# A four-layer graph network on one core: the edge attributes are transposed in the first layer and stored turned, instead of being transposed in the message layer

## The chip, the cores and the metric

One core of one Trainium2 chip. The metric is the device time of one execution of the whole kernel, in microseconds (us); it was taken in several runs, of which the median is given. Lower is better.

## What is computed

A graph of N = 3125 nodes and 50,000 edges, sorted by destination, goes through four layers with a layer norm ahead of each and a residual behind it:

```
x: (3125, 64)   src, dst: (50000,)   edge_attr: (50000, 32)
layer 0  typed:     agg[n] = sum over edges into n of  h[src] @ W[type],  16 types
layer 1  mean:      h[n] @ W_r + mean over edges into n of h[src] @ W_l
layer 2  message:   m = silu([h[src], h[dst], edge_attr] @ w1 + b1) @ w2 + b2
                    agg[n] = sum of m;  h[n] = LN(h[n] + mlp([h[n], agg[n]]))
layer 3  attention: 8 edge types, keys from h[src], h[dst] and active rules,
                    softmax over the edges into n, weighted sum of values
```

The part of `w1` that multiplies the edge attributes has 32 rows, so each edge needs one product of 32 numbers with a 32 x 64 matrix.

## The kernel before

**Tiles.** The sorted edges are cut into tiles of 128. A pair of an edge tile and a node tile (128 nodes) that it has edges into is a slot: 416 slots in G = 52 groups of SG = 8. The groups are also cut in four chunks, `PIECES` = (16, 16, 12, 8) groups. Every layer that sums over edges runs over the 52 groups. All five engines run their own program over them, in an order that is written out by hand, and meet in semaphores with a number per group.

**One group.** POOL gathers eight tiles of 128 rows (L583, one indirect DMA each) from a table in memory: row i of a tile is the table's row for edge i's source. They lie in a ring of eight groups; before it fills a place again it waits, in the first two layers, for PE's sum of an earlier group (`used`), in the message layer for DVE's adds (`edge_sum`). DVE makes the one-hots of a group (`oh`, L785: 128 edges by 128 nodes for each slot) in one of two buffers, for which it waits for the sum two groups back. PE multiplies the one-hots with the gathered rows and adds into the sums of the nodes in its own memory (eight matmuls by slot, recorded as sixteen; L1388 in the first two layers, L1353 in the message layer), and then signals `used`.

**The message layer** adds for each group: SP loads the slots' node numbers once for all partitions (`drow`, L518) and the edge attributes (`ea`, L514); DVE makes transposed one-hots from the former (`ohT`, L791); PE transposes the attributes (`ea_T`, two transposes, L1502, signal `eaT_ps`), ACT copies them to SBUF (`take_ea`, L1203, signal `eaT_sb`), and PE multiplies them with `w1c` (two matmuls, L1509) and adds the destination's part by the one-hots (L1511), signal `eb_ps`; DVE adds the gathered source part (L960, signal `edge_sum`), ACT applies Silu (L1209, signal `silu`), and PE sums (L1353). The programs run ahead of each other: at group g PE transposes for g + 2, makes the edge products of g + 1 and sums g. The program's names for both the gathered tiles and the attributes are parts of one buffer, `flat`, in the records.

**The attributes' way to memory.** The message layer needs the attributes of whole edge tiles by slot. In the first layer, behind the gathers of groups 12, 22, 32 and 42 (`TAKE_EA`), POOL gathers one chunk's attributes (L594): each of up to 128 partitions gets one slot's 128 x 32 numbers, 16 KB. SP stores them as they are in `edge_attr_by_slot` (L497, four stores). The message layer loads them from there with the edges over the partitions: 1024 pieces of 128 B for a group.

**The first layer** gathers typed rows from a table of nodes by types, except in the first twelve groups (`WHOLE`), for which plain rows have been gathered ahead, and PE does transposes and typed products (`turned0`, `typed0`) while the table isn't there yet.

## Time and profile before

| | |
|---|---|
| median of 3 runs | 2665.6 us |
| lowest and highest | 2657.2, 2675.9 us |
| span of the profiled execution | 2690.8 us |
| busy: PE, DVE, ACT, POOL | 1523.2, 1051.5, 487.3, 1543.2 us |
| DMA packets, data moved | 159861, 159.26 MB |

The profiled execution is one more execution than the three of the median; nothing but its span is recorded of it, so that the rows of the trace are to be held against 2690.8 us. An engine's busy time is that of its instructions; a DMA that POOL or SP issues is not in their busy time except for POOL's building of an indirect DMA, which the rows show as an instruction of POOL.

The page of the profile cuts the span in slices; two of its rows, for orientation, are PE's and POOL's, where each digit is one fortieth of the span in tenths of busy time:

```
PE   5545332424478888765376667659553536445564
POOL 5447766764667777735566666662344556665620
```

The first layer's gathers lie in slices 3 to 10, the message layer's in 19 to 27, the last layer's from 33 on.

### The profile page before, as it was taken

To read this page: it belongs to the slowest core of one execution; us is meant where nothing else is said; L and a number is where in the kernel's file an instruction comes from. 1 tells how busy PE (TensorE), PEld (TensorE's weight loads), DVE (VectorE), ACT (ScalarE), POOL (GpSimd) and SP (SyncE) were. 2 spreads that over 40 slices of the span, in tenths; PEclk is the share of its full clock that TensorE was granted. 3 is DMA by queue.
4 is the path that set the end of the run, shared out by engine and by line. 5 is a ranking of instruction groups with operands and counts; after the bars stand their busy time and mean duration, and the time that the engine had idled before them with its cause. 6 is when DMAs were issued, how large, how long until landed. Compare 5 with 4: busy or idle time off the path is not lost.

```text
span 2690.8 us, 27765 instructions
## 1 busy us (share of the span) xinstructions
PE 1523.2 (57%) x8443; PEld 1343.0 (50%) x8443; DVE 1051.5 (39%) x2213; ACT 487.3 (18%) x1153; POOL 1543.2 (57%) x1509
## 2 busy tenths in 40 slices
PE   5545332424478888765376667659553536445564
PEld 2224332424367777765376666658332325435554
DVE  4446110111556565633122222223524634334467
ACT  2100000000356666501000000001211111001020
POOL 5447766764667777735566666662344556665620
PEclk8656555555677777766555655657656766666677
DMA  6432122120111111103122222222341212222210
GB/s 199 130 110 86 24 84 58 36 61 16 30 31 36 34 37 34 33 12 65 37 52 50 57 51 51 58 51 44 110 162 52 65 54 66 61 55 68 58 39 13
DMA packets 159861, 159.26 MB, mean 59 GB/s; under 512 B 108361, under 2 KB 111993, under 8 KB 158748
## 3 DMA queue, kind: packets, MB, share of 16 engines
q1 hardware_dynamic: 111372, 89.07, 11.7%
q0 software_dynamic: 48352, 68.42, 11.5%
q8 instruction: 79, 1.29, 0.2%
q14 instruction: 58, 0.48, 0.1%
HBM read 118.71 MB, written 46.06 MB: 61 GB/s over the span
## 4 chain that ended last, share of the span: by engine, by line
another core or an unknown queue 30%; DVE 21%; PE 17%; issue 16%; POOL 10%; DVEq 2%; ACT 1%; DMA 1%; SPq 1%; ACTq 0%; POOLq 0%
POOL flat L583 10%; DVE flat L824 7%; PE ps L1353 4%; DVE oh L785 2%; DVE oh L1043 2%; PE ps L1388 2%; PE ps L1511 2%; DVE msg L1034 2%; DVEq L333 1%; PE ps L1341 1%; DVE msg L960 1%; DVE ohT L791 1%; PE ps L1325 1%; PE ps L1509 1%
## 5 line engine op out<-in xcount | busy, mean ns | idle before, releaser
L583 POOL DMA_INDIRECT flat<-table,flat x1061 | 1122.8, 1058 | 639.7 <-issue 314.7
L1388 PE MATMUL ps<-flat,oh 128*128 x1664 | 328.9, 380 | 368.1 <-DVE oh L785 255.3
L785 DVE TENSOR_TENSOR oh<-iota_n,drel 128x1024 f32<-128x1024 f32 x156 | 190.1, 1223 | 867.8 <-remote 605.0
L1388 PEld LDWEIGHTS ps<-flat,oh 128*128 128x128 f32 x1664 | 314.3, 291 | 394.7 <-issue 392.7
L583 POOL DMA_INDIRECT flat<-table,tile_idx x359 | 346.7, 966 | 267.9 <-DVE base L1037 140.2
L1353 PE MATMUL ps<-msg,oh 128*128 128x64 f32 x832 | 173.3, 393 | 156.5 <-ACT msg L1209 135.4
L1353 PEld LDWEIGHTS ps<-msg,oh 128*128 128x128 f32 x832 | 166.6, 304 | 160.4 <-issue 160.4
L1366 PE MATMUL ps<-uvT,flat 128*128 128x192 bf16 x2200 | 229.3, 275 | 25.7 <-ACT flat L1191 17.2
L1366 PEld LDWEIGHTS ps<-uvT,flat 128*128 128x128 bf16 x2200 | 219.8, 112 | 34.6 <-issue 29.3
L1576 PE MATMUL ps<-qn,ohT 128*128 x832 | 159.0, 349 | 124.9 <-issue 104.0
L1511 PEld LDWEIGHTS ps<-uvT,ohT 128*128 128x128 f32 x832 | 178.3, 291 | 64.3 <-issue 48.9
L1576 PEld LDWEIGHTS ps<-qn,ohT 128*128 128x128 f32 x832 | 143.4, 258 | 132.7 <-issue 132.1
L824 DVE TENSOR_TENSOR flat<-flat,iota_node 128x1536 bf16<-128x1536 f32 x110 | 193.2, 1757 | 3.0
L1511 PE MATMUL ps<-uvT,ohT 128*128 x832 | 166.1, 361 | 48.2 <-issue 48.2
L1187 ACT ACTIVATE flat<-flat,iota_node 128x512 bf16<-128x512 f32 x220 | 146.8, 714 | 170.8 <-DMA flat<-tile_source 105.5
L1585 PE MATMUL ps<-flat,oh 128*128 128x65 f32 x704 | 115.0, 329 | 70.7 <-DVE oh L1043 45.5
L1585 PEld LDWEIGHTS ps<-flat,oh 128*128 128x128 f32 x704 | 112.6, 248 | 76.2 <-issue 76.2
L1191 ACT ACTIVATE flat<-flat 128x512 bf16<-128x512 bf16 x220 | 126.4, 621 | 3.5
L1260 ACT COPY flat<-flat 128x64 f32 x416 | 65.8, 241 | 271.7 <-DMA flat<-table,tile_idx 209.3
L1032 DVE COPY rule_e<-ps 128x32 f32<-128x32 f32 x52 | 9.8, 188 | 269.2 <-remote 225.1
L1203 ACT COPY flat<-ps 128x256 f32<-128x256 f32 x52 | 19.3, 373 | 528.4 <-remote 360.4
L1509 PE MATMUL ps<-flat 128*128 128x256 f32 x208 | 105.0, 602 | 9.7 <-issue 9.4
(320 smaller groups left out, 1481.9 us busy)
## 6 DMA issues: line engine op xcount, KB each, us to landing
table<-flat SPq DMA_DIRECT2D x52, 512.0 KB
drow<-slot_node SPq DMA_DIRECT2D x104, 256.0 KB
flat<-table,flat POOLq DMA_INDIRECT x1061
flat<-edge_attr_by_slot SPq DMA_DIRECT2D x52, 128.0 KB
edge_attr_padded<-edge_attr SPq DMA_DIRECT2D x1, 6250.0 KB
flat<-table,tile_idx POOLq DMA_INDIRECT x359
flat<-tile_source SPq DMA_DIRECT2D x22, 256.0 KB
edge_attr_by_slot<-flat SPq DMA_DIRECT2D x2, 2048.0 KB
```

What stands on the lines that cost most here:

```text
L583: nc.gpsimd.indirect_dma_start(dest(t % PLACES), None, table, at_).then_inc(tile_gat[k % TRING], 16)
L785: V.tensor_tensor(oh[:, b], iota_n[:].unsqueeze(1).broadcast_to([P, SG, P]), drel[:, g * SG:(g + 1) * SG].unsqueeze(2).broadcast_to([P, SG ...
L824: V.tensor_tensor(src_oh[:, m % BINS, 0:ON_DVE, :], src_row[:, b].unsqueeze(1).broadcast_to([P, ON_DVE, PICK * P]), iota_node[:, CH * c:CH ...
L1187: last = A.activation(src_far[:, k - ON_DVE], src_row[:, q % 2], ACT.Square, bias=iota_node[:, t:t + 1], scale=-1.0)
L1191: last = A.activation(src_oh[:, m % BINS, k, :], src_far[:, k - ON_DVE], ACT.Relu, bias=1.0, scale=-1.0)
L1353: last = T.matmul(acc[:, bass.ds(n[j] * D, D)], oh[:, b, j, :], rows_[:, j, :], start=False, stop=True, skip_group_check=True)
L1366: last = T.matmul(picked_ps[b][:, j], src_oh[:, m % BINS, k, j * P:(j + 1) * P], h_parts[:, :, t, :], start=(t == 0 and j % 2 == 0), stop= ...
L1388: last = T.matmul(acc[:, bass.ds(n[j] * pitch + shift, width)], oh[:, b % 2, j, :], got[:, bass.ds(place[j], width)], start=False, stop=Tr ...
L1509: T.matmul(eb[b % 2][:, 256 * q:256 * q + 256], eaT[:, b % 2, q, :], w1c.rearrange("p s d -> p (s d)"), start=True, stop=False, skip_group ...
L1511: last = T.matmul(eb[b % 2][:, j * D:(j + 1) * D], ohT[:, b % 2, j, :], v[:, bass.ds(n[j], 1), :].rearrange("p t d -> p (t d)"), start=Fal ...
L1576: last = T.matmul(qr_ps[g % 2][:, j // 4, j % 4], ohT[:, b % 2, j, :], qn_room[:, bass.ds(n[j] * QR, P)], start=True, stop=True)
L1585: last = T.matmul(acc[:, bass.ds(n[j] * PITCH + SHIFT, W)], oh[:, b % 2, j, :], values[:, bass.ds(lw * SG + j, 1), :].rearrange("p s d -> ...
```

## The change

It has three parts.

- The message layer loses `ea_T` on PE, `take_ea` on ACT and their two semaphores. SP's load `ea_in` fills `eaT` itself, with 1 KB for each partition, from a new array `edge_attr_turned` that has one block of 128 x 256 for each group. It waits for `eb_ps`, the edge products two groups back, where it had waited for the transposes two groups back (`eaT_ps`).
- The first layer gets `turn_ea` on PE: 58 steps of four transposes, by way of four rooms in PSUM, and 58 copies on ACT. A chunk has eight steps (`TURNS`) that read the gathered rows with a stride of 32 numbers and turn them from "slot by edge" to "edge by slot" for one attribute each, and then one step for two groups that turns blocks of 4 slots by 32 attributes to the form that the product wants. Two steps stand behind the sum of a group, for the groups from TAKE_EA + 2 on: 14 to 21, 24 to 31, 34 to 40 and 44 to 49. The steps of a group wait for the copy of four steps back.
- SP's four stores become 26 of 256 KB, each behind its step's copy; POOL's gather of the next chunk's attributes waits for the chunk's eighth step (`ea_turned`) instead of for the store; PE waits for the last copy before it goes on to the nodes.

```diff
@@ SP
             for c in range(SC):
-                sp.wait_ge(s("ea_taken"), 16 * (c + 1))
-                sp.dma_start(ea_slot_d[START[c]:START[c] + ROWS_OF[c], :], ea_rows[0:ROWS_OF[c], :]).then_inc(s("ea_slot_out"), 16)
+                for k in range(PIECES[c] // 2):
+                    pair_ = FIRST[c] // 2 + k
+                    sp.wait_ge(s("ea_moved"), ea_steps_before(c) + TURNS + k + 1)
+                    sp.dma_start(eaT_d[2 * pair_:2 * pair_ + 2].rearrange("g p k -> p g k"), turned_ea[:, pair_ % 2, :].rearrange("p (g k) -> p g k", g=2)).then_inc(ea_out[pair_ % 2], 16)
...
             def ea_in(g, b):
-                sp.wait_ge(s("eaT_ps"), g + 1)
-                sp.dma_start(ea[:, b, :].rearrange("e (s d) -> e s d", s=SG), ea_slot_d[g * SG:(g + 1) * SG, :].rearrange("s (e d) -> e s d", d=ED)).then_inc(eas[b], 16)
+                sp.wait_ge(s("eb_ps"), g + 1)
+                sp.dma_start(eaT[:, b].rearrange("p q k -> p (q k)"), eaT_d[g]).then_inc(eas[b], 16)
@@ POOL, in the first layer, at the groups of TAKE_EA
                     if c:
-                        pool.wait_ge(s("ea_slot_out"), 16 * c)
+                        pool.wait_ge(s("ea_turned"), ea_steps_before(c - 1) + TURNS)
@@ ACT, first layer
+            for i, (c, k) in enumerate(EA_STEPS):
+                act.wait_ge(s("ea_turned"), i + 1)
+                if k < TURNS:
+                    A.copy(by_edge[:, 0:ROWS_OF[c], 4 * k:4 * k + 4], room[i % 4].rearrange("p (d s) -> p s d", d=4)[:, 0:ROWS_OF[c], :]).then_inc(s("ea_moved"), 1)
+                else:
+                    pair_ = FIRST[c] // 2 + k - TURNS
+                    if pair_ >= 2:
+                        act.wait_ge(ea_out[pair_ % 2], 16 * (pair_ // 2))
+                    A.copy(turned_ea[:, pair_ % 2, :], room[i % 4]).then_inc(s("ea_moved"), 1)
@@ ACT, message layer
-            def take_ea(g, b):
-                act.wait_ge(s("eaT_ps"), g + 3)
-                act.wait_ge(s("eb_ps"), g + 1)
-                A.copy(eaT[:, b % 2], tp[b % 2][:, 0:2 * P].rearrange("p (q k) -> p q k", q=2)).then_inc(s("eaT_sb"), 1)
-
             def step2(g, b, left):
-                if left > 2:
-                    take_ea(g + 2, b)
@@ PE, first layer
+            def turn_ea(i, c, k):
+                if i == 0:
+                    pe.wait_ge(s("ahead_read"), 4 * WHOLE[0] + 1)
+                if i >= 4:
+                    pe.wait_ge(s("ea_moved"), i - 3)
+                if k == 0:
+                    pe.wait_ge(s("ea_taken"), 16 * (c + 1))
+                if k == TURNS:
+                    pe.wait_ge(s("ea_moved"), i)
+                n = ROWS_OF[c]
+                for j in range(4):
+                    if k < TURNS:
+                        last = T.transpose(room[i % 4][:, j * P:j * P + n], ea_rows[0:n, :].rearrange("s (e d) -> s d e", d=ED)[:, 4 * k + j, :], ident[0:n, 0:n])
+                    else:
+                        at_ = 4 * (4 * (k - TURNS) + j)
+                        last = T.transpose(room[i % 4][:, j * P:(j + 1) * P], by_edge[:, at_:at_ + 4, :].rearrange("p s d -> p (s d)"), ident[:])
+                last.then_inc(s("ea_turned"), 1)
...
                     if l == 0 and g + 2 < WHOLE[0]:
                         turned0(g + 2)
+                    if l == 0:
+                        for i in ea_steps_at(g):
+                            turn_ea(i, *EA_STEPS[i])
@@ PE, message layer
-            def ea_T(g, b):
-                pe.wait_ge(eas[b % 2], 16 + (g - b % 2) * 8)
-                for q in range(2):
-                    last = T.transpose(tp[b % 2][:, q * P:(q + 1) * P], ea[:, b % 2, q * P:(q + 1) * P], ident[:])
-                last.then_inc(s("eaT_ps"), 1)
-
             def edges2(g, b, n):
                 pe.wait_ge(s("ohT"), g + 3)
-                pe.wait_ge(s("eaT_sb"), g + 1)
+                pe.wait_ge(eas[b % 2], 16 + (g - b % 2) * 8)
...
-                if left > 2:
-                    pe.wait_ge(s("eaT_sb"), g + 1)
-                    ea_T(g + 2, b + 2)
```

The order of instructions shows it at three places. First, PE in the first layer, between the sum of group 18 and that of group 19, before the change. The names: `flat` is here the buffer of the gathered rows, `ps` PE's sums, TENSOR_LOAD a read of the slots' numbers, ISA the setting of an address.

```order
L1388 MATMUL ps<-flat,oh 128x65
L333 TENSOR_LOAD flat x2
L1388 ISA [waits tiles_gathered3,ahead_done,oh]
L1388 MATMUL ps<-flat,oh 128x65
L1388 ISA
L1388 MATMUL ps<-flat,oh 128x65
```

The same place with the change:

```order
L1422 MATMUL ps<-flat,oh 128x65
L1401 MATMUL ps<-ident,flat 128x128 [waits ea_moved]
L1401 MATMUL ps<-ident,flat 128x128 x3
L1401 MATMUL ps<-ident,flat 128x128 [waits ea_moved]
L1401 MATMUL ps<-ident,flat 128x128 x3
L334 TENSOR_LOAD flat x2
L1422 ISA [waits tiles_gathered3,ahead_done,oh]
L1422 MATMUL ps<-flat,oh 128x65
```

Eight transposes and two waits for ACT's copies have come between the two sums. The second place is PE in the message layer, from the end of one group's sum to the edge products of a later one, before the change:

```order
L1353 MATMUL ps<-msg,oh 128x64
L333 TENSOR_LOAD flat
L1502 MATMUL ps<-ident,flat 128x128 [waits ea_in0,eaT_sb]
L1502 MATMUL ps<-ident,flat 128x128
L1509 MATMUL ps<-flat 128x256 [waits eaT_sb,ohT,edge_sum]
L1511 ISA
```

And with it:

```order
L1368 MATMUL ps<-msg,oh 128x64
L334 TENSOR_LOAD flat
L1541 MATMUL ps<-flat 128x256 [waits ea_in1,ohT,edge_sum]
L1543 ISA
L1543 MATMUL ps<-uvT,ohT 128x64
```

The two transposes are gone, and the products wait for the load itself where they waited for ACT's copy. The third place is SP at the beginning of the message layer, before the change:

```order
L518 DMA drow<-slot_node 128x1024 [waits ohT,ea_slot_out]
L514 DMA flat<-edge_attr_by_slot 128x8x32 [waits eaT_ps]
L518 DMA drow<-slot_node 128x1024 [waits ohT]
L514 DMA flat<-edge_attr_by_slot 128x8x32 [waits eaT_ps]
```

And with it:

```order
L532 DMA drow<-slot_node 128x1024 [waits ohT,turned_ea_out1,turned_ea_out0]
L528 DMA flat<-edge_attr_turned 128x256 [waits eb_ps]
L532 DMA drow<-slot_node 128x1024 [waits ohT]
L528 DMA flat<-edge_attr_turned 128x256 [waits eb_ps]
```

The loads keep their places; what the attributes' load waits for is the edge products in place of the transposes, and it stands ahead of the next group's `drow` on the same queue.

## Rows read from the trace of the kernel before

**Rows 1.** The page, its top and part 1: busy us (share of the span) x instructions

```profile
span 2690.8 us, 27765 instructions
...
PE 1523.2 (57%) x8443; PEld 1343.0 (50%) x8443; DVE 1051.5 (39%) x2213; ACT 487.3 (18%) x1153; POOL 1543.2 (57%) x1509
```

**Rows 2.** Windows by stage: stretch, length, busy PE PEld DVE ACT POOL, PEclk, DMA share, GB/s

```profile
186.00:652.00 466.00, 173.14 (x751) 151.03 (x750) 98.28 (x80) 1.87 (x7) 328.63 (x324) 0.52 0.22 53
1237.00:1816.00 579.00, 360.44 (x1624) 340.37 (x1624) 126.69 (x427) 43.66 (x88) 374.11 (x372) 0.55 0.26 52
1816.00:1880.00 64.00, 58.61 (x336) 55.99 (x335) 25.32 (x94) 8.92 (x17) 16.85 (x15) 0.70 0.24 46
```

**Rows 3.** Timeline of 1464 to 1482: start, duration, engine, operation, count [idle before <-releaser]

```profile
1464.93 3.62 PE L1353 MATMUL ps<-msg,oh 128*128 128x64 f32 x16
...
1468.34 0.63 PE L1502 MATMUL ps<-ident,flat 128*128 128x128 f32 x2
...
1475.04 0.94 POOL L583 DMA_INDIRECT flat<-table,flat  x1 [0.30 <-issue]
...
1478.40 1.22 DVE L785 TENSOR_TENSOR oh<-iota_n,drel 128x1024 f32<-128x1024 f32 x1 [15.73 <-remote]
1478.44 0.37 ACT L1203 COPY flat<-ps 128x256 f32<-128x256 f32 x1 [15.77 <-remote]
...
1480.95 1.21 POOL L583 DMA_INDIRECT flat<-table,flat  x1 [4.97 <-DVE msg L960]
```

**Rows 4.** Waits of POOL; windows 1230:1845, 186:282 (two rows), 282:652, 2147:2581

```profile
POOL flat L583 <- DVE msg L960: 95.7, 18, 18.1
...
POOL flat L583 <- issue: 22.9, 62, 4.3
POOL flat L583 <- remote: 4.4, 1, 4.4
...
POOL flat L583 <- remote: 25.1, 5, 7.6
...
POOL flat L583 <- DVE base L1037: 103.7, 16, 19.7
```

**Rows 5.** Timeline of the first layer, around 464 and behind its last gather

```profile
464.19 1.23 DVE L785 TENSOR_TENSOR oh<-iota_n,drel 128x1024 f32<-128x1024 f32 x1 [38.68 <-remote]
464.43 1.82 POOL L583 DMA_INDIRECT flat<-table,flat  x1 [5.59 <-remote]
...
652.54 17.32 PE L1388 MATMUL ps<-flat,oh 128*128 x80 [21.61 <-DVE oh L785]
```

**Rows 6.** Timeline at the start of the message layer

```profile
1273.37 0.37 PE L1502 MATMUL ps<-ident,flat 128*128 128x128 f32 x1 [2.42 <-issue]
...
1331.90 1.21 POOL L583 DMA_INDIRECT flat<-table,flat  x1 [18.06 <-DVE msg L960]
```

**Rows 7.** Timeline behind POOL's last gather of the message layer

```profile
1848.54 0.63 PE L1502 MATMUL ps<-ident,flat 128*128 128x128 f32 x2
1848.97 1.06 PE L1509 MATMUL ps<-flat 128*128 128x256 f32 x2
```

**Rows 8.** Waits of PE in 1237:1880, and the timeline of one attributes' load

```profile
PE ps L1353 <- ACT msg L1209: 135.4, 25, 10.0
...
1236.99 0.43 SPq L514 DMA_DIRECT2D flat<-edge_attr_by_slot  x1
...
1240.72 0.41 PE L1502 MATMUL ps<-ident,flat 128*128 128x128 f32 x2 [0.74 <-DMA flat<-edge_attr_by_slot]
```

**Rows 9.** Timeline of a shorter pause of the message layer

```profile
1677.79 1.23 DVE L785 TENSOR_TENSOR oh<-iota_n,drel 128x1024 f32<-128x1024 f32 x1 [14.31 <-remote]
...
1680.35 1.21 POOL L583 DMA_INDIRECT flat<-table,flat  x1 [3.55 <-DVE msg L960]
```

**Rows 10.** SP's queue in 1430:1780 and 2222:2550: packets, MB, share of 16 engines

```profile
q1 hardware_dynamic: 33152, 11.01, 15.9%
...
q1 hardware_dynamic: 3744, 6.82, 7.6%
```

More of the change, by code:

```diff
@@ L66, in network @@
         drel_d = dram("slot_node", (SLOTS, P), bf16)
-        ea_slot_d = dram("edge_attr_by_slot", (SLOTS, P * ED))
+        eaT_d = dram("edge_attr_turned", (G, P, SG * ED))
         src_d = dram("tile_source", (SC * P, P))
@@ L190, in network @@
         ohT = sb("ohT", [P, 2, SG, P])
-        ea_room = early(P, [2 * SG * ED])
-        ea = ea_room.rearrange("p (b k) -> p b k", b=2)
+        eaT = early(P, [2, 2, P])
         src_oh_at = taken[0]
-        eaT = early(P, [2, 2, P])
         msg = sb("msg", [P, 2, SG, D])
@@ L208, in network @@
         assert 2 * R0 * D == 2 * SG * P
+        by_edge = flat[:, taken[0]:taken[0] + P * ED].rearrange("p (s d) -> p s d", d=ED)
         pack = early(P, [SC, 4, P], i32)
@@ L276, in network @@
         pre2 = early(P, [NT, D])
+        turned_ea = pre.rearrange("p t d -> p (t d)")[:, 0:4 * SG * ED].rearrange("p (b k) -> p b k", b=2)
         src_rows = early(P, [SC, P])
@@ L325, in network @@
         eas = [s("ea_in0"), s("ea_in1")]
+        ea_out = [s("turned_ea_out0"), s("turned_ea_out1")]
         tab = [s(f"table_out{b}") for b in range(4)]
@@ L376, in network, with ea_steps_before, ea_steps_at @@
         TAKE_EA = (12, 22, 32, 42)
+        TURNS = ED // 4
+        def ea_steps_before(c):
+            return sum(TURNS + n // 2 for n in PIECES[0:c])
+        EA_STEPS = [(c, k) for c in range(SC) for k in range(TURNS + PIECES[c] // 2)]
+        def ea_steps_at(g):
+            return [i for i, (c, k) in enumerate(EA_STEPS) if g == TAKE_EA[c] + 2 + k // 2]
         def groups(eng, step):
@@ L519, in drow_in @@
                              .rearrange("p (s k) -> p s k", s=SG)).then_inc(drows[b], 16)
-            sp.wait_ge(s("ea_slot_out"), 16 * SC)
+            for b in range(2):
+                sp.wait_ge(ea_out[b], 16 * G // 4)
             for g in range(G):
@@ L901, in _ @@
             link(V.tensor_tensor(pre2, pre2, row("L2_gnn_b3"), ALU.add))
+            for b in range(2):
+                dve.wait_ge(ea_out[b], 16 * G // 4)
             for k, (t0, t1) in enumerate(HALVES):
@@ L912, in _ @@
             dve.wait_ge(s("drel_out"), 16 * SC)
-            dve.wait_ge(s("ea_slot_out"), 16 * SC)
             dve.sem_inc(s("stage_over"), 1)
@@ L1198, in _ @@
             take_transposed(hT)
-            def take_ea(g, b):
-                act.wait_ge(s("eaT_ps"), g + 3)
-                act.wait_ge(s("eb_ps"), g + 1)
-                A.copy(eaT[:, b % 2], tp[b % 2][:, 0:2 * P].rearrange("p (q k) -> p q k", q=2)).then_inc(s("eaT_sb"), 1)
             def step2(g, b, left):
-                if left > 2:
-                    take_ea(g + 2, b)
                 act.wait_ge(s("edge_sum"), g + 2)
                 A.activation(msg[:, b % 2], msg[:, b % 2], ACT.Silu).then_inc(s("silu"), 1)
-            take_ea(0, 0)
-            take_ea(1, 1)
             groups(act, step2)
@@ L1295, in _ @@
             pe.sem_inc(s("used"), 2)
-            pe.sem_inc(s("eaT_ps"), 2)
             pe.sem_inc(s("eb_ps"), 2)
@@ L1458, in _ @@
             gathered_sums(0)
+            pe.wait_ge(s("ea_moved"), len(EA_STEPS))
             node_transposes(h[:], *both("h", 3))
@@ L1528, in step2 @@
                 sum_into_nodes(b % 2, n, msg[:, b % 2])
-            ea_T(0, 0)
-            ea_T(1, 1)
             edges2(0, 0, tiles_of[0])
```

## The prediction

> **What bounds the kernel now.** I read four views in this order: the page's busy times, the windows by stage, the waits of POOL, and the timeline of one pair of groups. POOL and PE are each busy for 57% of the span, so neither explains it alone [rows 1]. By stage [rows 2] the two parts that the change touches are the gathers of the first layer (186 to 652) with the sums behind them, and the message layer: 579 us until POOL's last gather, then 64 us in which PE finishes. One gather takes 0.94 us and the next starts 0.30 us later, so a group of eight costs POOL 10 us, and with a pause of 4.97 us a pair of groups takes some 25 [rows 3]. POOL is the pacemaker there, and what it loses are its pauses: 18 of them, 95.7 us, between one run of gathers and the next [rows 4].
>
> What ends a pause is seen in the timeline [rows 3]. PE's sum of a group runs from 1464.93 for 3.62 us, so it ends at 1468.6, and PE goes on at once with transposes and edge products. But DVE, which waits for the semaphore of that sum (`used`) and for nothing else, starts its one-hots only at 1478.40, 9.8 us later, and ACT, which waits for the transposes of 1468.34, starts its copy at 1478.44. Both start 2.4 us after POOL's sixteenth gather has ended (1475.04 plus 0.94). Only DVE's adds, behind them, let POOL go on, at 1480.95: a pause of 4.97 us. So while POOL gathers without a break, PE's finished work becomes known late. The first layer has the same: one-hots that wait for a sum start at 464.19, 38.68 us after DVE's last work, and POOL resumes at 464.43 after 5.59 us [rows 5]. At the start of the message layer it is visible in PE itself: a transpose of 0.37 us (1273.37) stands 2.42 us behind the record before it, 2.8 us from start to start, where two of them take 0.63 us elsewhere [rows 3], and that stretch ends in the longest pause, 18.06 us [rows 6]. I can't name the mechanism from this trace. What I can count is how often it bites: 18 pauses in 52 groups with 38 PE matmuls each by the code (1976; the two windows have 1624 and 336 records [rows 2], a few are missing), 5 pauses in the 41 groups or so of the first layer after its twelfth (282 to 652), with 16 each, and 1 pause named so in the 96 us before, where the typed products of the first twelve groups come on top [rows 4].
>
> **Message layer: what goes.** Per group two transposes of PE, one copy of ACT (0.37 us [rows 3]), and two handovers (PE to ACT, ACT to PE). PE's two transposes cost little of its time: the product behind them starts 0.43 us later (1848.54 to 1848.97), with the clock at 0.70 in that window [rows 2, 7].
> (a) While POOL gathers, this time is off the path: PE waits for ACT's Silu 135.4 us in the layer, and what the transposes themselves wait for, the attributes' load, ends 0.74 us of waiting once [rows 8]. Worth 0.
> (b) After POOL's last gather PE is the bound (busy 58.61 of 64 us [rows 2]), for some six groups of which four or five still have transposes: 4.5 times 0.43. **Minus 2.**
> (c) In the slow stretch at the start two transposes stand between the sum of one group and the edges that the next adds need. At 2.8 us each they cost 5.6 us. **Minus 3**, bounds 0 and 5.6.
> (d) The pauses. They have two usual lengths: 4.97 us [rows 3] and 3.55 us [rows 9], 1.4 us apart. In the short one DVE was released 1.0 us after POOL's last gather (1676.80 to 1677.79), in the long one 2.4. Between the first release of a pair and its second PE has 54 matmul records (sum, transposes, edges, sum: 16, 2, 20, 16); after the change 52. If the late release is a queue of finished work, two records fewer bring it forward by something between nothing and the 1.4 us of the two lengths, for the 17 pauses behind the first. The third of the bounds is that all pauses go: 95.7 us. Against a large gain speaks the last layer: it has no attributes and no transposes at all and still 16 pauses with 103.7 us [rows 4]. I take 0.8 us for each of 17, the middle of 0 and 1.4 rounded up: **minus 14**, bounds 0 and 95.7.
>
> **Message layer: what moves.** The attributes' load now waits for `eb_ps`, the edge products two groups back, where it waited for transposes two groups back; and the one-hot load of the next group is queued behind it on SP. By the pair of [rows 3] the edges of a pair end at about 1473 and are known at 1478.4; the load that this frees lands some 4 us later (the load issued with the group at 1236.99 was what PE waited for until 1240.72 [rows 8]), and the products that read it start a sum, an edge block and a sum later, two sums of 3.62 us alone [rows 3]. So over 7 us stand against some 4. The one-hot load behind it has the same slack. Cost 0; if the cover failed in each group it would be some 2 us a group, 100 us, which I take up in the rivals' tail, not in the sum.
> The load itself shrinks from 1024 pieces of 128 B to 128 of 1 KB. In 350 us of the layer SP's queue moved 33152 packets and held 15.9% of the DMA engines; in 328 us of the last layer, without attributes, 3744 packets and 7.6% [rows 10]. That work goes from engines that are busy for a quarter of the time and are waited for by nobody: 0. The Trainium skill, page "DMA: Bandwidth & Descriptors", section Specifications, says that a transfer needs pieces of at least 512 B for line rate. By that rule the load gets cheaper, and if the layer followed its DMA time the saving would be the 8.3 points between the two shares, some 50 us of 643. The trace gives the rule no place to act, because only 0.7 us of waiting ends on that load; I keep it as a reason for the fast rival, no more.
>
> **First layer: what is added.** 58 steps of four transposes, 232 in all, in groups 14 to 49, two steps behind the sum of a group; 58 copies of 128x512 on ACT, which is idle there (1.87 us busy of 466 [rows 2]), at twice the 0.37 us of one half as wide [rows 3], 43 us in all beside the gathers; 26 stores of 256 KB in place of 4 of up to 2 MB; and waits: PE for ACT's copies, POOL for the eighth step of a chunk before it gathers the next chunk's attributes.
> (e) Where PE is not the bound, 8 transposes a group at 0.21 us (half of the 0.43) are 1.7 us in a group of 10 to 11, with PE 37% busy (173 of 466) [rows 2]: 0. Half of them read their rows with a stride of 32 elements, which no row of this trace does. Bounds: 0.21 us, as contiguous ones, and three times that, 5.1 us a group; even so PE fits beside 10 us.
> (f) At the end PE is the bound: five sums stand back to back behind the last release (652.54, 17.32 us) [rows 5]. The steps of groups 47 to 49, and perhaps of 46, now stand between them: 24 to 32 transposes at 0.21 us. **Plus 6.** PE's new wait for the last copy costs nothing, since two sums follow the last step. SP's loads of the next layer are queued behind the last store; it comes two sums ahead of this layer's end, and the first of them is wanted only behind the normalisation of the nodes: 0.
> (g) Release of finished work. 24 records a group in place of 16. After the twelfth group 5 pauses with 25.1 us stand in 370 us; in the 96 us before, with about 25 records a group, 1 with 4.4 and one more that the view puts under issue, of 4.3 [rows 4]. The denser part thus has two pauses in 11 groups, 0.18 a group, the thin part 5 to 7 in 40, some 0.13 to 0.17. The difference, up to 0.06 for 29 groups, is 1.7 pauses of 4.4 us: **plus 8**. Bounds: 0, and the message layer's rate of 18 in 52, 0.35 a group, which makes 6 more pauses of 5 us, 30.
> (h) POOL's wait for the eighth step: its tile gathers of that group had waited for the sum just ahead of the step, 10 us earlier. Between 0 and 5 us at each of three places; I take 0, since the gatherer would have paused a group later anyway.
>
> **The sum.** Minus 2, minus 3, minus 14, plus 6, plus 8: minus 5 on a profiled span of 2690.8 us. That execution is 0.9% above the median of the runs, 2665.6, and there is nothing else to take its surroundings from; I scale the difference with it and predict 2661 us. A measurement of this kernel, with runs from 2657.2 to 2675.9, tells about 1% from no change.
>
> **The rivals.**
> A, clearly faster: the pauses of the message layer go for the most part, because PE no longer stands between its sums with a handover to ACT, and because 46,600 small packets leave the queues. For it: in the pauses ACT's copy and DVE's one-hots are released within 0.04 us of each other [rows 3], so the copy is part of what is late. Against: the last layer's 16 pauses. Half of 95.7 us, with (b) and (f) to (g): minus 5 more than minus 35 and down to minus 85: 2575 to 2630, say 2615.
> B, slower: the added steps bring the first layer into the state of [rows 6]. It is one mechanism: PE issues one record in 2.8 us while POOL gathers, the eighth step waits for a copy that waits for a release, the sums behind it stand, and POOL pauses for 18 us in place of 5. It happens if the steps are dense enough to fill whatever fills at the start of the message layer; four chunks at 13 us more give plus 52, together with the rest 2705 to 2720. From two such places on it outweighs the message layer's gain. Against: the first twelve groups of this layer have as many records and show no such stretch.
> C, the message layer gains nothing but (b), since its rhythm is POOL's and the last layer's equals it, and the first layer pays (f) and (g): plus 12, 2677. That is within 1%, as is my forecast.
> D, that the change doesn't do what it says: the transposes are gone from the message layer, as the order of instructions shows, so this is only the case of DMA time that nobody waited for; it gives C's time.
>
> **How the numbers follow.** Forecast and C together 0.60, A 0.25, B 0.15. Faster by over 1% 0.25, within 1% 0.60, slower 0.15. The range goes from 2612, which leaves out the lower part of A, to 2702, which leaves out most of B.
>
> **What the changed profile would show.** The windows of the message layer 15 to 20 us shorter, its pauses fewer than 18 or shorter than 95.7 us in sum; no wait for the attributes' load in PE's list; the same pace of about 25 us a pair. In the first layer 232 more transposes, POOL's pauses at 35 to 40 us in sum in place of 29.5, and 23 us in place of 17.3 behind the last release. Wrong would be the forecast if the first layer's pauses grow by more than 30 us, if transposes with the long stride take over 1 us each, or if the message layer's pauses vanish.

## The result, and the profile after

The changed kernel takes 2683.45 us in the median of 20 runs, the kernel before, timed with it, 2667.46 us in the median of 20. The ratio is 1.0073, with a 95% interval of 1.0042 to 1.0103: slower by 0.7%. That is inside what I had called no change and inside the range, but I had forecast the other sign (minus 5 us), and the interval excludes it. One of the two profiled executions is unusual and the other isn't: the kernel before was profiled at a span of 2690.8 us, far above its median, the changed one at 2681.3, near its own. So the two spans say nothing of the change, and what follows compares stretches. The experiments further down ran on two chips, the first and the third series on one and the second on another, and the kernel before has another median on each; every run is compared with the kernel before on its own chip. Some executions fell in a slower state of the chip: the ratios leave them out, the medians don't.

The top of the page and its part 1, changed kernel:

```profile
span 2681.3 us, 27979 instructions
...
PE 1565.1 (58%) x8571; PEld 1381.6 (52%) x8571; DVE 1051.3 (39%) x2213; ACT 500.8 (19%) x1159; POOL 1538.0 (57%) x1509
```

PE has 128 matmuls more (8571 against 8443 in [rows 1]; 232 were added and 104 taken away), and is busy 42 us longer. At 0.24 us a transpose (1.94 us for eight, L1401 at 324.96) 128 of them are worth 31 us, so some of the 42 us are something else. The windows by stage, the same three as [rows 2] (stretch, length, busy time of PE, PEld, DVE, ACT, POOL, then PE's granted clock, DMA share, GB/s):

```profile
186.00:652.00 466.00, 208.22 (x993) 182.88 (x992) 101.94 (x84) 30.54 (x61) 326.63 (x324) 0.56 0.21 50
1237.00:1816.00 579.00, 379.20 (x1579) 354.85 (x1580) 128.54 (x433) 27.16 (x43) 380.86 (x377) 0.51 0.23 52
1816.00:1880.00 64.00, 54.20 (x227) 51.19 (x225) 20.58 (x70) 4.44 (x7) 10.79 (x11) 0.50 0.15 40
```

The second row is the one to read. PE executed 1579 matmuls where it had executed 1624, and was busy longer for them, 379 us in place of 360. The granted clock had been 0.55 there and is 0.51; in the third window it had been 0.70 and is 0.50, the lower level, all the time. POOL's waits, in the order of [rows 4], for windows 1225:1845, 282:655 (three rows) and 2147:2581 (two rows):

```profile
POOL flat L598 <- DVE msg L976: 88.5, 18, 16.9
...
POOL flat L598 <- remote: 29.7, 7, 5.8
POOL flat L598 <- PE ps L1422: 6.0, 1, 6.0
POOL flat L609 <- remote: 4.0, 1, 4.0
...
POOL flat L598 <- DVE base L1053: 78.3, 15, 9.2
...
POOL flat L598 <- ACT flat L1276: 5.2, 1, 5.2
```

The message layer's pauses have hardly changed (88.5 us against 95.7). Those of the first layer after its twelfth group are 39.7 us in sum against 25.1. The last layer, in which no instruction differs, has 83.5 us in its two rows against 103.7 before, 20 us less: so much do pauses differ from one execution to another.

Then what had no row ahead of the prediction: the time from POOL's last gather of the message layer to its first of the next layer. It stands in brackets behind POOL's next gather, as the idle time before it. Timeline, first of the kernel before, then of the changed one; the rows of PE are the sums of groups behind POOL's last gather:

```profile
1845.13 3.62 PE L1353 MATMUL ps<-msg,oh 128*128 128x64 f32 x16
1853.98 3.62 PE L1353 MATMUL ps<-msg,oh 128*128 128x64 f32 x16
1861.95 1.95 PE L1353 MATMUL ps<-msg,oh 128*128 128x64 f32 x16
1867.13 1.99 PE L1353 MATMUL ps<-msg,oh 128*128 128x64 f32 x16 [0.40 <-ACT msg L1209]
1872.34 1.99 PE L1353 MATMUL ps<-msg,oh 128*128 128x64 f32 x16 [0.40 <-ACT msg L1209]
...
1920.29 0.95 POOL L571 DMA_INDIRECT uvT<-table,flat  x1 [82.23 <-DMA table<-h]
```

```profile
1862.85 3.62 PE L1368 MATMUL ps<-msg,oh 128*128 128x64 f32 x16
1871.38 3.62 PE L1368 MATMUL ps<-msg,oh 128*128 128x64 f32 x16
1879.91 3.62 PE L1368 MATMUL ps<-msg,oh 128*128 128x64 f32 x16
...
1934.59 0.94 POOL L586 DMA_INDIRECT uvT<-table,flat  x1 [104.36 <-DMA table<-h]
```

From one sum to the next is one group. Before, the first group took 8.85 us and the later ones 5.2, since the granted clock rose in the middle: it is 0.50 from 1840 to 1860 and 1.00 from 1865 to 1880. In the changed kernel each takes 8.53 us to the end. The 0.32 us that the removed transposes saved per group at the half clock is there; the 3.3 us per group that the full clock had given is gone. The stretch is 22 us longer: 104.36 in place of 82.23. Two things are in these 22 us. PE had seven sums left behind POOL's last gather before and eight in the changed kernel, which is one group or 8.5 us; the other 13 or so are four groups at 3.3 us, the clock.

### The profile page after: what moved, and what is told of

Its sections match the earlier page's. It is cut to its first block, busy times and chain, and to the rows that moved or that the text cites. A ratio compares the mean times of both kernels' runs of the same rounds, so it can differ in the third digit from the quotient of the medians.

```text
span 2681.3 us, 27979 instructions
## 1 busy us (share of the span) xinstructions
PE 1565.1 (58%) x8571; PEld 1381.6 (52%) x8571; DVE 1051.3 (39%) x2213; ACT 500.8 (19%) x1159; POOL 1538.0 (57%) x1509
## 4 chain that ended last, share of the span: by engine, by line
another core or an unknown queue 33%; DVE 22%; PE 19%; issue 17%; POOL 5%; DVEq 2%; ACT 1%; DMA 1%; SPq 1%; ACTq 0%; POOLq 0%
DVE flat L839 6%; POOL flat L598 5%; PE ps L1368 4%; PE ps L1422 3%; DVE oh L800 3%; PE ps L1543 2%; DVE oh L1059 2%; DVE msg L1050 1%; DVEq L334 1%; PE ps L1541 1%; PE ps L1603 1%; DVE ohT L806 1%; PE ps L1340 1%; PE ps L1356 1%
## 5 line engine op out<-in xcount | busy, mean ns | idle before, releaser
L1422 PE MATMUL ps<-flat,oh 128*128 x1664 | 316.9, 362 | 279.2 <-DVE oh L800 146.9
L1422 PEld LDWEIGHTS ps<-flat,oh 128*128 128x128 f32 x1664 | 303.8, 277 | 303.4 <-issue 300.3
L1368 PE MATMUL ps<-msg,oh 128*128 128x64 f32 x832 | 187.6, 419 | 119.8 <-ACT msg L1227 117.0
L1543 PEld LDWEIGHTS ps<-uvT,ohT 128*128 128x128 f32 x832 | 198.9, 321 | 91.9 <-issue 75.8
L1368 PEld LDWEIGHTS ps<-msg,oh 128*128 128x128 f32 x832 | 180.8, 329 | 124.7 <-issue 124.7
L1543 PE MATMUL ps<-uvT,ohT 128*128 x832 | 186.6, 391 | 66.5 <-issue 66.4
L1227 ACT ACTIVATE msg<-msg 128x512 f32<-128x512 f32 x52 | 32.9, 632 | 636.1 <-DVE msg L976 514.8
L1612 PEld LDWEIGHTS ps<-flat,oh 128*128 128x128 f32 x704 | 108.7, 240 | 80.1 <-issue 80.0
L1541 PE MATMUL ps<-flat 128*128 128x256 f32 x208 | 119.3, 666 | 23.5 <-issue 22.9
```

The lines of the kernel that those rows point to most:

```text
L1368: last = T.matmul(acc[:, bass.ds(n[j] * D, D)], oh[:, b, j, :], rows_[:, j, :], start=False, stop=True, skip_group_check=True)
L1422: last = T.matmul(acc[:, bass.ds(n[j] * pitch + shift, width)], oh[:, b % 2, j, :], got[:, bass.ds(place[j], width)], start=False, stop=Tr ...
L1541: T.matmul(eb[b % 2][:, 256 * q:256 * q + 256], eaT[:, b % 2, q, :], w1c.rearrange("p s d -> p (s d)"), start=True, stop=False, skip_group ...
L1543: last = T.matmul(eb[b % 2][:, j * D:(j + 1) * D], ohT[:, b % 2, j, :], v[:, bass.ds(n[j], 1), :].rearrange("p t d -> p (t d)"), start=Fal ...
L1612: last = T.matmul(acc[:, bass.ds(n[j] * PITCH + SHIFT, W)], oh[:, b % 2, j, :], values[:, bass.ds(lw * SG + j, 1), :].rearrange("p s d -> ...
```

## The experiments

Three theories stood after this. **F**: the loss comes from the transposes and waits added in the first layer. **M**: it comes from the message layer, where PE, with its transposes gone, is granted the higher clock (2.4 GHz, 1.00 in the rows; the lower is 1.2 GHz, 0.50) less. **W**, against M: PE's work sets the end of the layer and the clock differs between two executions by chance.

### First series: each half alone

The first run has the first layer of the changed kernel and the message layer of the one before:

```diff
+        ea_slot_d = eaT_d.rearrange("g p k -> (g p k)").rearrange("(t k) -> t k", k=P * ED)
...
             def ea_in(g, b):
-                sp.wait_ge(s("eb_ps"), g + 1)
-                sp.dma_start(eaT[:, b].rearrange("p q k -> p (q k)"), eaT_d[g]).then_inc(eas[b], 16)
+                sp.wait_ge(s("eaT_ps"), g + 1)
+                sp.dma_start(ea[:, b, :].rearrange("e (s d) -> e s d", s=SG), ea_slot_d[g * SG:(g + 1) * SG, :].rearrange("s (e d) -> e s d", d=ED)).then_inc(eas[b], 16)
```

with `ea_T` and `take_ea` as they were.

> The first layer of the changed kernel with the message layer of the kernel before, which reads the stored bytes as if they lay by slot (so the edge attributes in it are permuted numbers; everything else is computed). Theory F (the loss comes from the 232 added transposes and their waits in the first layer): the whole loss is here, ratio about 1.007, some 16 us over the kernel before. Theory M (it comes from the message layer, where PE keeps the half clock behind POOL's last gather and has a group more left to do): ratio 1.000, within 5 us; the stretch from POOL's last gather of the message layer to the first one of the next layer is near the 82 us of before and not near the 104 us of the changed kernel. The windows of the first layer show POOL's pauses at some 42 us, as in the changed kernel, where before had 34, in both theories.

Measured: 2669.75 us against 2671.49, ratio 1.0000 (0.9958 to 1.0042); POOL's pauses in the first layer 38.9 us. The second run is the opposite, the first layer of before and the message layer of the changed kernel; its first layer stores as before, into the array that the message layer reads:

```diff
+        eaT_d = dram("edge_attr_turned", (G, P, SG * ED))
+        ea_slot_d = eaT_d.rearrange("g p k -> (g p k)").rearrange("(t k) -> t k", k=P * ED)
```

> The first layer of the kernel before (its four stores go as they are into the new array) with the message layer of the changed kernel, so that the attributes it uses are permuted numbers; everything else is computed. Theory F: the message layer gains its few us, ratio 0.995 to 1.000. Theory M: the whole loss is here, ratio about 1.007, with a PE clock of 0.50 in nearly all of the message layer, gathers that end some 9 us earlier than before and a stretch of over 100 us from the last gather to the next layer's first.

Measured: 2682.59 us against 2671.49, ratio 1.0032 (0.9984 to 1.0081). The interval holds both theories' numbers. The traces tell them apart better; the window 1840 to 1880 of the kernel before, then of the first run and of the second the same window and POOL's first gather behind the message layer:

```profile
1840.00:1880.00 40.00, 38.38 (x228) 36.53 (x226) 18.05 (x67) 6.28 (x12) 0.00 (x0) 0.74 0.16 31
```

```profile
1840.00:1880.00 40.00, 36.67 (x242) 34.69 (x242) 16.41 (x58) 7.89 (x15) 0.00 (x0) 0.81 0.11 21
...
1911.65 0.95 POOL L589 DMA_INDIRECT uvT<-table,flat  x1 [86.10 <-DMA table<-h]
```

```profile
1840.00:1880.00 40.00, 38.68 (x167) 36.87 (x167) 10.89 (x39) 5.50 (x10) 0.00 (x0) 0.50 0.05 14
...
1913.53 0.95 POOL L570 DMA_INDIRECT uvT<-table,flat  x1 [94.19 <-DMA table<-h]
```

With the transposes in the message layer the clock there is 0.81 and the stretch 86.10 us, without them 0.50 and 94.19. That is M. Expected for the second run was over 100 us, but POOL's last gather ended 19 us earlier than in the kernel before (at 1819 in place of 1838; 9 had been expected) and only seven sums were left behind it, eight in the first run. The count of groups left therefore isn't the cause: from the last gather to the end of the last sum PE took 55.6 us for seven groups in the second run and 47.1 us for eight in the first.

The third puts two transposes back into each group of the changed kernel's message layer, of rows that lie there anyway:

```diff
+                for q in range(2):
+                    T.transpose(tp[b % 2][:, (q % 2) * P:(q % 2 + 1) * P], h[:, 2 * (q % 2):2 * (q % 2) + 2, :].rearrange("p t d -> p (t d)"), ident[:])
                 if left > 1:
                     pe.wait_ge(s("edge_sum"), g + 1)
```

> The changed kernel, and in each group of the message layer PE does two transposes of node rows, at the place of the former ones, whose result nobody reads or waits for. Theory M in the form that the clock follows PE's work: the granted clock of the message layer goes back from 0.51 towards 0.56 and the time back to that of the kernel before, ratio 1.000, 16 us under the changed kernel. If the former handover to ACT mattered and not the work, or by theory F: ratio 1.008, the changed kernel's time plus one or two us.

Measured: 2677.08 us, ratio 1.0017 (0.9977 to 1.0056). Its clock from 1332 to 1800 was 0.53 (0.55 before, 0.51 changed), its stretch 91.55 us, and the window 1840 to 1880 still 0.50. Here the clock rose late: the first sum of 1.95 us in place of 3.62 starts at 1881.68, 49 us behind the last gather, where it came after 24 us in the kernel before and after 20 us in the first run. The time and the stretch moved towards those of before, the former by 8 us where 16 had been expected: half a confirmation.

The fourth is the changed kernel again.

> The changed kernel once more, for a second profile of it and for the size of the change on this chip. All theories: ratio 1.004 to 1.010. Theory M: again a PE clock near 0.50 between POOL's last gather of the message layer and the layer's end, and over 100 us from that gather to the next layer's first; if this profile has some 80 us there, the 104 us were chance and theory M is weakened.

Measured: 2684.90 us, ratio 1.0049 (1.0012 to 1.0086). Its window, and its stretch:

```profile
1840.00:1880.00 40.00, 40.00 (x172) 38.38 (x171) 13.89 (x49) 2.52 (x4) 0.00 (x0) 0.50 0.13 34
...
1928.57 0.94 POOL L586 DMA_INDIRECT uvT<-table,flat  x1 [96.90 <-DMA table<-h]
```

The half clock repeats itself. The stretch had been expected at over 100 us and isn't; this execution had seven groups left, the first one eight.

A trace is one execution, but the mean granted clock of the whole execution is on record for every timed one. On this chip, the third series with it, it is:

| | executions | mean granted clock |
|---|---|---|
| before | 46 | 0.630 |
| turning in the first layer, transposes kept (run 1) | 6 | 0.636 |
| transposes taken out, first layer of before (run 2) | 6 | 0.619 |
| changed kernel, both (runs 4 and 9) | 18 | 0.625 |
| changed kernel, two transposes put back (run 3) | 6 | 0.637 |

The standard error of each is at most 0.0014. Taking the transposes out of the message layer costs 0.011 of the mean clock, whichever first layer stands beside it, and putting two back returns it. So the loss of clock is an effect of the change and not chance. The mean doesn't say where in the execution the clock is lost.

### Second series: more work for PE

Theories M and W differ most where PE is given more to do. The fifth run is the kernel before with each pair of transposes made three times:

```diff
-                for q in range(2):
+                for q in (0, 1) * 3:
                     last = T.transpose(tp[b % 2][:, q * P:(q + 1) * P], ea[:, b % 2, q * P:(q + 1) * P], ident[:])
```

> The kernel before, whose message layer makes each pair of transposes three times, six per group in place of two. Theory M (what the message layer lost with its two transposes is the higher clock that they helped PE to): the clock of the message layer is at or above the 0.56 of before, the stretch behind POOL's last gather at or below the 82 us of before, and the time within 8 us of before, ratio 0.995 to 1.002, although PE has 208 transposes more. Theory W (PE's work sets the tail, and the longer tail of the changed kernel is chance): four transposes at 0.21 us in each of some eight groups behind the last gather and in some of the rest, 7 to 20 us more, ratio 1.003 to 1.008.

Measured: 2636.28 us against 2633.37 on this chip, ratio 1.0017 (0.9984 to 1.0049). Clock 0.65 from 1332 to 1800, stretch 74.64 us. The sixth is the third run with `range(8)`.

> The changed kernel with eight transposes of node rows in each group of the message layer, whose results nobody reads, where the third run of this study had two. Theory M: the clock of the message layer rises to 0.56 or more, the stretch from POOL's last gather to the next layer's first falls from about 100 us to 85, and the time from the changed kernel's 2684 to 2665 to 2675. Theory W: 8 times 0.21 us more in each group of the tail, 14 us more than the changed kernel.

Measured: 2643.19 us, ratio 1.0028 (0.9991 to 1.0066). Clock 0.66 from 1332 to 1800 and 0.79 behind that, stretch 75.26 us. The seventh uses another kind of work, and puts it where PE waits:

```diff
                 pe.wait_ge(s("oh"), 2 * G + g + 1)
+                ones_ = oh[:, b % 2].rearrange("p s k -> p (s k)").bitcast(bf16)
+                for q in range(4):
+                    T.matmul(tp[q % 2], ones_[:, 0:P], ones_[:, 512:1024], start=True, stop=True, skip_group_check=True)
                 pe.wait_ge(s("silu"), g + 1)
```

> The changed kernel with four bf16 matmuls of 512 columns (one-hots by one-hots, nobody reads the result) in each group of the message layer, ahead of the wait for ACT's Silu, in which PE otherwise stands for 117 us in the layer. An estimate of 0.4 us for each at the half clock makes 1.7 us a group. Theory M: the clock of the message layer goes to 0.70 or above, the last groups take some 6 us each where they took 8.53, the stretch behind the last gather is under 85 us, and the time is 2655 to 2670. Theory W: 14 us slower than the changed kernel.

Measured: 2646.52 us, ratio 1.0024 (0.9985 to 1.0064). Clock 0.64, then 0.70 and 0.90; groups at the end 5.24 us each; stretch 85.65 us. The clock while POOL gathers (0.70 had been expected) and, by a little, the stretch missed what M had said. The eighth has the same lines under `if g >= 42`.

> The same four wide matmuls, only in the last ten groups (42 to 51) of the message layer. If the loss of the changed kernel lies in the clock behind POOL's last gather, this one gives it back alone: that stretch under 85 us in place of 97 to 104, time 2660 to 2672, while the windows ahead of it keep a clock of 0.50. By theory W it is some 14 us slower than the changed kernel.

Measured: 2640.56 us, ratio 1.0010 (0.9974 to 1.0047); clock 0.51 up to 1800, then 0.75 and 0.84; stretch 83.35 us.

More work brought more clock: over whole executions the mean is 0.660, 0.668 and 0.661 in runs 5 to 7, against 0.640 for the kernel before on the same chip. The eighth, with idle work in ten groups only, has 0.637, and there is no changed kernel on this chip to hold it against. The stretches are 74.64 to 85.65 us, where the two kernels with two transposes had 82.23 and 86.10 and the changed one 96.90 and 104.36; but neither kernel was profiled on this chip. The times don't decide. W had forecast 7 to 20 us more for the fifth run, which has 3 by the medians and 4.5 by the ratio, with an interval that reaches 13. The ratios of the other three lie between 1.001 and 1.003, and each interval holds 1. Nor did the higher clock make any of these kernels faster than the one before. That the changed kernel's own ratio on this chip wasn't known was a gap in the series, and the third one closes it.

### Third series: the changed kernel with and without the clock, on one chip

> The changed kernel on the chip of the three that follow. Theory M: ratio 1.004 to 1.008, a PE clock of 0.50 to 0.52 in the windows from 1332 to 1880, and 55 to 65 us of PE work behind POOL's last gather of the message layer, where the kernels with transposes had 35 to 47.

> The changed kernel with the four wide idle matmuls in groups 42 to 51, the same as in the second series, now on the chip of the changed kernel itself. Theory M: 8 to 16 us below the changed kernel of this series, ratio to before 0.999 to 1.003, and at most 47 us of PE work behind the last gather. If it stands less than 4 us below the changed kernel, the clock of the tail is not where its time went.

> The first layer of before, the message layer of the changed kernel (on permuted attributes, as in the second run) and the four wide idle matmuls in groups 42 to 51. The remaining price of the first layer is the difference to the run before this one: by the traces so far 3 to 5 us. Theory M: ratio to before 0.996 to 1.001, better than before by the few us that the message layer's handovers are worth.

The twelfth run has the line of the fifth from group 42 on:

```diff
-                for q in range(2):
+                for q in (0, 1) * (3 if g >= 42 else 1):
```

> The kernel before, with each pair of transposes made three times from group 42 on: computes all that the reference does, and is the version to which theory M points as the fastest that needs no turning. Expected: ratio 0.995 to 1.000, at most 40 us of PE work behind the last gather in place of 43.7 and 47.1. If PE's work counts and not its clock, 3 to 7 us slower than before.

Measured, each against 2664.38 us of the kernel before on this chip:

| | us | ratio | 95% interval | POOL's stretch behind the message layer | PE's work in it, to the end of the last sum |
|---|---|---|---|---|---|
| changed (9) | 2686.40 | 1.0059 | 1.0026 to 1.0093 | 102.63 | 64 |
| changed, four idle matmuls in ten groups (10) | 2661.30 | 0.9979 | 0.9951 to 1.0007 | 75.35 | 37 |
| message part only, with the same (11) | 2659.70 | 0.9987 | 0.9949 to 1.0025 | 84.42 | 46 |
| before, transposes thrice from group 42 (12) | 2661.35 | 0.9983 | 0.9949 to 1.0018 | 76.15 | 37 |

The changed kernel and the tenth run differ in 40 matmuls whose result nobody reads. They make it 25 us faster by the medians and 21 by the ratios, and the two intervals don't touch. The window 1840 to 1880, first of the ninth run and then of the tenth:

```profile
1840.00:1880.00 40.00, 37.63 (x161) 36.20 (x161) 13.87 (x50) 3.16 (x5) 0.00 (x0) 0.50 0.14 43
```

```profile
1840.00:1880.00 40.00, 38.35 (x285) 34.65 (x286) 18.83 (x65) 7.05 (x12) 0.00 (x0) 0.96 0.12 34
...
1841.55 1.89 PE L1368 MATMUL ps<-msg,oh 128*128 128x64 f32 x16
1843.28 0.65 PE L1541 MATMUL ps<-flat 128*128 128x256 f32 x2
1843.76 1.00 PE L1543 MATMUL ps<-uvT,ohT 128*128 x8
1844.60 0.65 PE L1541 MATMUL ps<-flat 128*128 128x256 f32 x2
1845.09 1.00 PE L1543 MATMUL ps<-uvT,ohT 128*128 x8
1846.14 0.81 PE L1559 MATMUL ps<-oh 128*128 128x512 bf16 x3
1846.79 1.89 PE L1368 MATMUL ps<-msg,oh 128*128 128x64 f32 x16
...
1910.33 0.94 POOL L586 DMA_INDIRECT uvT<-table,flat  x1 [75.35 <-DMA table<-h]
```

The lines between 1841.55 and 1846.79 are one group, idle matmuls included: 5.24 us, where the changed kernel takes 8.53 us without them. The sum of a group takes 1.89 us where it had taken 3.62. In 40 us PE executes 285 matmuls in place of 161, at the same busy share. The stretch is 27 us shorter, and the run 21 to 25 us. With the two other runs that have these matmuls (83.35 us in the eighth, 84.42 in the eleventh) the mean stretch is 81.0 us, against 101.3 in three profiles of the changed kernel, still 20 us less: nothing else is needed to account for the difference. Theory W is out, and with it F as the main cause.

The eleventh run against the tenth shows what the turning in the first layer costs once the clock is out of it: 1.6 us by the medians, 2 us the other way by the ratios, where 3 to 5 had been expected; and the first run's ratio is 1.0000. All have an uncertainty of some 10 us, so no cost is seen, and one of a few us isn't excluded. The twelfth shows that the kernel before has the same to gain: with a little more for PE to do at the end its stretch falls from 82.23 (86.10 in the first run) to 76.15 us. The ninth, the eleventh and the twelfth came out in the ranges that M had given; the tenth gained more than its 8 to 16 us (its ratio had been put at 0.999 to 1.003). Of the last three the tenth and the twelfth compute the whole reference. Both lie some 3 us under the kernel before, which their intervals don't tell from none; both beat the changed kernel.

## Why the prediction was wrong

**Term (b), the end of the message layer, is the step that failed.** It said minus 2 us: PE bounds that stretch, and two transposes fewer per group save 0.43 us for four or five groups. That PE bounds the stretch is right, and a saving is in the rows (8.53 us a group in place of 8.85, 0.32). But it priced the removed work alone, and held the clock at what it was. The clock depends on the work (run 2 and run 10 show it from both sides), and the stretches behind the last gather are 104.36, 96.90 and 102.63 us in the three profiles of the changed kernel, mean 101.3, and 82.23 and 86.10 in the two profiles with the old message layer, mean 84.2. So the term is plus 17 and not minus 2, which is the size of the whole result (16 us between the medians). Between 1 and 2 us of the 17 are the count of groups left, 8, 7 and 8 against 7 and 8; five profiles are few, and the tenth run's 21 to 25 us are the better evidence. The row to ask was in [rows 2]: 0.55 while POOL gathers and 0.70 in the last window mean that the kernel before stood part of the time at the upper level, with no margin shown. I had even used the clock of 0.70 to price the transposes.

**Term (d), the pauses of the message layer, was too large.** Minus 14 was forecast, from a queue of finished work that two records fewer would shorten. POOL's wait for the adds is 95.7, 88.1, 81.7 and 89.2 us in the four profiles with the attributes by slot (before, runs 1, 5 and 12), mean 88.7; in the ten with the changed message layer it is 69.1 to 90.5, mean 83.7. That is minus 5, less than it varies by from one execution to another. The evidence against the gain, the last layer with as many pauses and no transposes, was in the text, and should have weighed more than the 1.4 us between two lengths of a pause.

**Term (c)** is not seen: the longest pause is 16.9, 18.0 and 17.7 us in the changed kernel, 18.1 before.

**Term (g), the first layer's pauses, was right in sign and of the right size.** Forecast plus 8. POOL's waits from 190 to 660 for finished work sum to 43.3, 40.7 and 36.3 us in the three profiles of the changed kernel and to 25.0 to 43.3, mean 36.1, in all nine that turn in the first layer; in the five with the old first layer (before, runs 2, 5, 11 and 12) to 27.5 to 32.9, mean 30.0. That is plus 6. The size is partly luck: the prediction had taken the upper end of its own difference ("up to 0.06" pauses a group) for the value. **(h)**, for which I took 0, is a part of it, the row of 4.0 us at L609; two more of the nine profiles have such a row, of 5.4 and 5.7 us.

**Term (e) was right.** The view of groups by form for PE in the changed first layer:

```profile
L1401 PE MATMUL ps<-ident,flat 128*128 128x128 f32 x104 | 24.4, 398 | 54.2 <-ACT flat L1193 35.6 <-issue 18.5
L1398 PE MATMUL ps<-ident,flat 128*128 128x128 f32 x64 | 15.0, 362 | 18.3 <-issue 18.1
```

L1398 reads with the stride of 32 numbers, L1401 without it: 15.0 us for 64 and 24.4 for 104, 0.23 us each. The stride costs nothing here. PE stood 33.3 us once for a copy of ACT (the 35.6 us are that and 2.3) and POOL was not delayed by as much, so PE's room there is real.

**Term (f)**, plus 6 at the end of the first layer, isn't seen. From the layer's last gather to the next layer's first POOL stood 31.6 to 41.0 us in the five profiles with the old first layer, mean 37.0, and 31.5 to 48.1 in the nine with the new one, mean 37.3. In the first profile of the changed kernel the clock was 0.84 from 660 to 670, where before it had been 0.50, so that here the added work may have paid for itself as it did in the message layer; that was not tried.

**The load** that waits for `eb_ps` cost nothing, as forecast: no row of PE's waits in the changed message layer names it. The DMA share fell from 0.26 to 0.23 in the layer, and the time didn't follow it.

**The rivals.** A fell with (d). B's mechanism, in which a step waits for a copy that waits for a release, did occur (the 33.3 us, and 40.2 and 34.8 us in runs 6 and 7). Behind the layer's twelfth group POOL had no pause over 6.0 us in the first profile, and none over 9.4 us in any, where B had 18. (A is misadded at its lower end: 2665.6 less 85 is 2581 and not 2575.) C named the size, plus 12, with the first layer as its cause; the runs show that cause to be small. None of my rivals had the clock in it, and that is the second fault: the slower case was put only where work was added.

With the measured terms the sum is plus 17 (b), minus 5 (d), plus 6 (g and h): plus 18. The timed runs say 16 (the medians) to 19 (the ratio).

## What to carry to other kernels

Where PE bounds a stretch and its granted clock stands between the two levels, price a change of its work at both levels first: an instruction taken away can cost more than it took, and one added can give more. Here 40 idle matmuls in ten groups gave the changed kernel 21 to 25 us, about what it had lost on that chip (16 to 22). There is no more to be had this way here: the kernel before with added transposes (run 12) isn't measurably faster than it was. Look at the stretch behind the pacemaker's last instruction by itself, and at its clock in more than one profile; it was some 85 to 100 us of 2690, and the result was in it. And run the changed kernel in every series of experiments on it, or the series tells only half.

## What the runs showed of the hardware

A busy PE doesn't have the full clock for that alone. In the changed kernel:

```profile
1840.00:1880.00 40.00, 40.00 (x170) 38.20 (x169) 14.70 (x50) 3.17 (x5) 0.00 (x0) 0.50 0.11 36
```

Its records fill all of the 40 us, as they do from 1837 to 1895, and the granted clock is 0.50, that is 1.2 GHz, throughout. In the tenth run they fill 38.35 of 40 us, and it is 0.96. The Trainium skill, page "TensorE: Matmul & The Clock Gate", Part 1, says that the clock is set by how busy the PE has been recently, and that activity releases the throttle. The second half agrees with the runs: wherever a kernel and the same with added PE work were on one chip, the mean granted clock of the whole execution was higher with it (0.630 to 0.636 in run 1, 0.625 to 0.637 in run 3, 0.640 to 0.660 in run 5, 0.626 to 0.634 in run 10, 0.630 to 0.634 in run 12). The first half doesn't, if busy is the share of time with a matmul on record, since a full record left the clock at the lower level for 58 us. What it is about the added work that counts, these runs don't separate: eight f32 transposes a group raised the clock (0.66 and 0.79), as did four wide bf16 matmuls, while two transposes went with 0.74 and 0.81 from 1840 to 1880 in the kernels with attributes by slot and with 0.50 in the third run, where it rose only at 1881. In the four profiles without transposes or idle work (the changed kernel's three and run 2) every sum behind POOL's last gather is at the lower level. When the clock rises in a full stretch, and why, is open.

While POOL gathers, PE's clock is of little account: from 1332 to 1800 it was 0.50 to 0.66 in these kernels, and POOL's pauses don't follow it (81.7 us at 0.65, 80.2 at 0.66, 84.4 at 0.50). Why PE's finished work becomes known late while POOL gathers is as open as it was in the prediction.
